# All of the second routed layer's shared expert beside the scatter, and the combination of routed results alone behind the expert loop

## The reference

```python
def _L1_ffn_ref(x, sg_w, su_w, sd_w, router_w, routing_bias, wg, wu, wd):
    xt = x.reshape(-1, H)
    shared = jax.nn.silu(xt @ sg_w.T) * (xt @ su_w.T) @ sd_w.T
    logits = xt @ router_w.T + routing_bias
    probs = jax.nn.sigmoid(logits)
    topk_p, topk_idx = jax.lax.top_k(probs, TOP_K)
    topk_p = topk_p / jnp.sum(topk_p, axis=-1, keepdims=True)
    ...
    h = jax.nn.silu(g) * u
    y = jnp.einsum('tei,ehi->teh', h, wd)
    routed = jnp.einsum('te,teh->th', w, y)
    return (shared + routed).reshape(orig_shape)
...
x = x + jnp.tanh(g_ffn[1]) * _L1_ffn_ref(_layernorm(x, axis=-1), ...)
```

## Time and profile before

| what | value |
|---|---|
| median of 3 runs | 1859.33 us (1855.94 to 1867.62) |
| the profiled execution | 1858.6 us |
| its span, first to last instruction | 1856.8 us |
| mean granted clock of TensorE | 0.878 of full speed |
| PE busy | 1455.4 us (78% of the span) |
| DVE, ACT, POOL busy | 1087.2, 894.4, 698.4 us |

### The profile page before, as it was taken

How to read it: one execution, slowest core, us unless ns; L and a number is a source line. 1 busy time by engine, 2 the same in 40 slices (tenths; PEclk the granted TensorE clock), 3 DMA queues, 4 the chain that set the end, 5 groups by cost and what they waited for, 6 DMA issues and landing times. The chain is left out here.

```text
span 1856.8 us, 31205 instructions
## 1 busy us (share of the span) xinstructions
PE 1455.4 (78%) x10050; PEld 1280.1 (69%) x10050; DVE 1087.2 (59%) x2502; ACT 894.4 (48%) x1907; POOL 698.4 (38%) x678
## 2 busy tenths in 40 slices
PE   1699982399999999758998369999855944463898
PEld 0457772399999999635787359999854842153687
DVE  6356643277777777455755426777553456777444
ACT  4244440377777777325552126777423515454242
POOL 2222103454444454542212423444541840045244
PEclk8899985699999999879997679999988977785799
DMA  8000004256465565220001305777420010001001
GB/s 290 1 1 1 1 10 172 84 199 236 183 238 213 203 238 193 73 71 1 1 1 35 128 33 178 236 228 231 125 66 26 1 50 1 0 29 53 1 13 35
DMA packets 75565, 179.95 MB, mean 97 GB/s; under 512 B 11776, under 2 KB 58112, under 8 KB 66256
## 3 DMA queue, kind: packets, MB, share of 16 engines
q1 hardware_dynamic: 56816, 149.91, 23.2%
q0 software_dynamic: 6144, 16.79, 2.8%
q10 hardware_dynamic: 12512, 12.06, 1.9%
HBM read 150.16 MB, written 28.57 MB: 96 GB/s over the span
## 5 line engine op out<-in xcount | busy, mean ns | idle before, releaser
L1386 POOL TENSOR_TENSOR l0m_e_DL<-l0m_e_DN,l0m_e_DH 128x256 fp32r<-128x256 f32 x184 | 200.0, 1088 | 218.1 <-ACT l0m_e_DH L1257 218.1
L1204 PE MATMUL PS<-l0m_e_CH,l0m_e_UH 128*128 128x256 f32 x736 | 210.8, 286 | 1.5 <-DVE l0m_e_CL L1345 1.5
L1204 PE MATMUL PS<-l0m_e_CH,l0m_e_UL 128*128 128x256 f32 x736 | 209.0, 284 | 0.0
L1204 PE MATMUL PS<-l0m_e_CL,l0m_e_UH 128*128 128x256 f32 x736 | 208.9, 284 | 0.0
L1317 DVE TENSOR_TENSOR l0m_e_UL<-l0m_e_U,l0m_e_UH 128x512 fp32r<-128x512 f32 x184 | 126.9, 690 | 45.8 <-ACT l0m_e_UH L1248 45.8
L1386 POOL TENSOR_TENSOR l1m_e_DL<-l1m_e_DN,l1m_e_DH 128x256 fp32r<-128x256 f32 x92 | 96.3, 1047 | 151.7 <-ACT l1m_e_DH L1257 151.7
L1329 DVE SCALAR_TENSOR_TENSOR l0m_e_HR<-PS,l0m_e_BU,l0m_e_SG 128x256 f32<-128x256 f32 x184 | 89.1, 484 | 104.8 <-ACT l0m_e_SG L1265 103.6
L1204 PEld LDWEIGHTS PS<-l0m_e_CH,l0m_e_UH 128*128 128x128 f32 x736 | 142.0, 193 | 1.9 <-ACT l0m_e_UH L1248 1.9
L1204 PEld LDWEIGHTS PS<-l0m_e_CL,l0m_e_UH 128*128 128x128 f32 x736 | 141.9, 193 | 0.0
L1204 PEld LDWEIGHTS PS<-l0m_e_CH,l0m_e_UL 128*128 128x128 f32 x736 | 141.8, 193 | 0.0
L1248 ACT CAST l0m_e_UH<-l0m_e_U 128x512 fp32r<-128x512 f32 x184 | 112.5, 612 | 57.3 <-PEq L1486 57.2
(11 more groups left out here) (468 smaller groups left out, 4526.9 us busy)
## 6 DMA issues: line engine op xcount, KB each, us to landing
l0m_e_U<-in_l_up SPq DMA_DIRECT2D x23, 2048.0 KB, 8.2
l0m_e_DN<-in_l_down SPq DMA_DIRECT2D x23, 1024.0 KB, 5.0
l1m_e_U<-in_l_up SPq DMA_DIRECT2D x23, 1024.0 KB, 7.1
l1m_e_DN<-in_l_down SPq DMA_DIRECT2D x23, 512.0 KB
rows_by_expert<-ZERO SPq DMA_DIRECT2D x1, 5888.0 KB, 27.4
l0m_e_ROW<-rows_by_expert SPq DMA_DIRECT2D x23, 256.0 KB, 5.0
results_by_expert<-l0m_e_Y ACTq DMA_DIRECT2D x23, 256.0 KB, 2.1
l1m_e_ROW<-rows_by_expert SPq DMA_DIRECT2D x23, 256.0 KB, 3.8
```

The costliest lines, as they stand in the source:

```text
L1204: ins = nc.tensor.matmul(hb(f)[:, a * SLOTS:(a + 1) * SLOTS], w[:, f % RING, k, a, :], x[:, j, k, :], start=(p == 0), stop=(p == len(passe ...
L1386: nc.gpsimd.tensor_tensor(DL[:, f % RING, :], DN[:, j, f, :], DH[:, f % RING, :].bitcast(F32), ALU.subtract).then_inc(s_dl, 1)
```

## The change

The first run takes all 16 rows (eight blocks of 256 tokens, 32 units), still beside the scatter. The third stage is a block of its own, in which POOL gathers as before and DVE has nothing but the combination's 16 rows in order. The arguments and counters that interleaved the combination with the shared run are gone. In the new file lines behind the edit have other numbers: 1605 becomes 1614, 1589 becomes 1598, 1635 becomes 1644, and so on.

```diff
                         s_sc = sem("l1m_scattered")
-                        shared.run("l1m_sh1", 0, B // 2, split=(SU, SD), on_sp=weights.first_tiles,
+                        shared.run("l1m_sh", 0, B, split=(SU, SD), on_sp=weights.first_tiles,
                                    on_pool=lambda pool: scatter(pool, Z, SLOT, s_sc))
                     expert_tiles("l1m_e", weights)
                 combine = Combine(c, "l1m_c", W12, SLOT)
-                shared.run("l1m_sh2", B // 2, B, on_pool=combine.gather, combine=combine)
+                with nc.Block() as block:
+                    @block.gpsimd
+                    def _(pool):
+                        combine.gather(pool)
+
+                    @block.vector
+                    def _(dve):
+                        for b in range(B):
+                            combine.sequence(dve, b)
+                        combine.end(dve)
...
-            def run(self, tag, lo, hi, split=None, on_sp=None, on_pool=None, combine=None):
+            def run(self, tag, lo, hi, split=None, on_sp=None, on_pool=None):
...
-                            done, combined = 0, 0
...
-                                    done = n * R
-                                if combine is not None and combined < lo + done:
-                                    if combined >= lo:
-                                        dve.wait_ge(s_out, combined - lo + 1)
-                                    combine.sequence(dve, combined)
-                                    combined += 1
...
-                            if combine is not None:
-                                dve.wait_ge(s_out, BLOCKS * R)
-                                for b in range(combined, B):
-                                    combine.sequence(dve, b)
-                                combine.end(dve)
```

## The result

| kernel | median | runs |
|---|---|---|
| before | 1862.94 us (1855.94 to 1867.62) | 20 |
| changed | 1871.26 us (1862.62 to 1874.86) | 20 |

The ratio is 1.0045, with a 95% interval of 1.0035 to 1.0055: the change costs some 8.4 us (6.5 to 10.2). The profiled execution of the changed kernel took 1874.4 us (span 1872.6).

A forecast was written before the change was run, and what follows sets the result against it. It took PE's chain, restarted at about 1083 after the scatter, to bound the first stage, and PE's chain again behind the loop. +34.8 - 26.1 = +8.7 us on 1858.6 gives 1867.3, for the median 1868 us; range 1857 to 1880.

The forecast's parts named there:

- the likely case: Whole kernel: a time within 1% (18.6 us) of before, given 0.82.
- sum of +8.7: Whole kernel: +34.8 us ahead of the expert loop and -26.1 behind it, +10.4 at the other end.
- Six units meet the scatter as before: First shared run: the first four blocks keep their order and stall as before, the sixth SG near 1083.
- The added blocks cost 4 x 8.69 = 34.8 us: Ahead of the expert loop: four more blocks after the scatter, 8.69 us each, all on the path.
- the closing: End of the shared run: a wait for the last HL, then 24 down matmuls, there once in either kernel.
- The loop unchanged: Expert loop: starts at 1147 instead of 1112, its 220 us unchanged.
- The last stage shrinks by 26.1 us: Behind the loop: without shared work the stage goes from 70.35 to 44.3 us.
- a pitch: Last stage: gathers follow one another without a pause, 1.256 us apart.
- POOL's closing: End of the last stage: POOL might leave later than DVE, 1.7 us extra not taken, making -24.4 the other end.
- The second rival: Last stage: DVE's adds slow POOL's gathers to 1.68 us each, 22.6 us longer, 1891 us; 8 in 100.
- The third: Added blocks ahead of the loop: PE at 1.2 GHz costs 30 us more, 1898 us; 3 in 100.
- The first: First stage: units keep their own pace through the scatter, sum -19.5, 1840 us; 4 in 100.

The follow-up runs named there:

- the second pair: Both kernels run again unchanged in a new series: before 1859.01 us, changed 1869.42 us, ratio 1.0049.
- without standing: Series where the shared expert keeps its pace while POOL makes indirect transfers; the kernel before took 1811.96, 1815.89 and 1815.76 us.
- x_two: Kernel before, scatter replaced by 32 direct SP transfers, second shared run in blocks of 512 tokens: 1830.08 us, one run.
- e_late: Kernel before with DVE's order alone changed, the combination's 16 rows behind the second run's last shared output: 1840.20 us, ratio 1.0121.
- x_both: Kernel before, scatter replaced by 32 direct SP transfers, all of the combination behind the last shared output: 1833.36 us.
- e_tok512b: Kernel before with the shared expert in blocks of 512 tokens in both runs: 1818.20 us, ratio 1.0021.

## Why the prediction was right, point by point

It gave 1868 us with a range of 1857 to 1880, and within 1% as the likely case; 1871.26 was measured, and the ratio of 1.0045 is inside that case. Its sum of +8.7 met +7.55 in the profiled pair, +8.15 by the two stages of the second pair, and 8.4 in the medians.

- *Six units meet the scatter as before, the sixth near 1083.* Right: 46.5 us behind the block's start, 44.9 before.
- *The added blocks cost 4 x 8.69 = 34.8 us.* The distance of a block was 8.70. The stage grew by 33.56, 1.2 less. The sixth SG came 1.6 us later after the stage's start than before, the five units behind it took 10.92 us instead of 12.26, and the closing was 1.5 shorter, which the prediction had counted as the same, "partly at the lower clock". From the run's last SG to the loop's first load, windows of before, and then of after:

```profile
1105.31:1112.55 7.24, 4.60 (x24) 4.42 (x24) 2.58 (x7) 1.08 (x3) 0.00 (x0) 0.76 0.00 0
```

```profile
1144.87:1150.59 5.72, 3.08 (x24) 2.91 (x24) 2.58 (x7) 1.08 (x3) 0.00 (x0) 1.00 0.00 0
```

  The same 24 matmuls took 4.60 us at a granted 0.76 and 3.08 at 1.00. In the changed kernel PE had been working without a pause for longer when it came to them.
- *The loop unchanged.* 220.81 against 220.52.
- *The last stage shrinks by 26.1 us.* It shrank by 26.30 (from 70.91 to 44.61 us; the prediction's 70.35 and 44.3 are cut at the block's start and end). Its terms: a pitch of 1.254 (1.256 predicted), and 2.83 us from the last issue to the last add (2.7). From the last add's start to DVE's end it was 0.94 us; the 1.13 of the prediction reach to the stage's end. The next transfer came at 1416.01, 4.48 of which came from the layers ahead; without them 1411.5, 1412.7 predicted. From DVE's end at 1414.07 to that transfer it was 1.94 us, 1.68 before: of the 1.7 us that POOL's closing might have added 0.3 is seen.
- *The second rival, DVE holding up the gather.* It didn't come: with 30 adds beside 32 gathers the longest took 0.99 us (one of before took 1.68). So here DVE's operations with two inputs in SBUF cost POOL nothing that shows.
- *The third, the lower clock.* It didn't come. The window of five added and old blocks in the changed kernel has PE busy all through at a granted 1.00:

```profile
1099.90:1143.43 43.53, 43.53 (x362) 43.27 (x361) 21.11 (x54) 15.66 (x44) 0.00 (x0) 1.00 0.01 1
```

- *The first, units that pass the scatter at their own pace.* In the series of the result it didn't come. In the three without standing it did, and then its price was wrong by its sign: it gave 1840, 19.5 us under before, and measured was +21 over. The step that failed is that it let the scatter swallow units in the changed kernel only, and set that against a kernel before whose PE stands. What lets PE pass the scatter lets it pass in both kernels, and the gather too.

That last point bears on the reason given, "because PE there is already late behind the scatter and nothing is left to hide it". For the series of the result it holds, and x_two shows it from the other side: take POOL's indirect transfers away and the first four blocks take 43.5 us. One thing in it is read too simply: "PE is late". PE's own rows of before show the matmuls of all six units over by 1052.24, and then a pause until the down products, which wait for DVE's HL of the fourth unit:

```profile
1052.24 0.28 PE L1605 MATMUL PS<-l1m_sh_CH,l1m_sh_UL 128*128 128x256 f32 x1
...
1062.64 0.42 DVE L1654 TENSOR_TENSOR l1m_sh_HL<-l1m_sh_HR,l1m_sh_HH 128x256 fp32r<-128x256 f32 x1
...
1063.15 0.55 PE L1589 MATMUL PS<-l1m_sh_DH,l1m_sh_HH 128*128 128x256 f32 x1 [10.64 <-issue]
```

ACT began the fifth and the sixth SG at 1061.88 and 1082.92, 11 and 31 us behind the last matmul of their units as PE's rows have it, where e_late has 0.3 us. Only from 1068.21 on does PE itself show single matmuls with pauses between them. So what comes late first is ACT's start, or the signal that it waits for; or the rows of PE are too early. The trace doesn't tell which, and the sum needs only that the sixth SG comes with the end of the scatter.

But the standing is no property of the kernel. Without it the four added blocks aren't hidden either but for 4.8 us, since the first four have used up 43.5 of the scatter's 48.3 (x_both, e_late), and there the second run was cheap: 54 - 44.6 = 9.4 us of the last stage for 34.8 us of PE's work. The sign is the same in both kinds of series, the size isn't: +8 and +21 us. The prediction read its rows in one series and didn't ask whether they would look the same in another. That the result came from a series of the same kind was luck on this point: in one without standing it would have been +1.1%, outside the likely case.

On the Trainium skill's sentence in "SBUF — State Buffer", section "Who interferes with whom", that a DMA never contends with a compute engine: x_two with its direct transfers and all series without standing agree with it. The waits of 21.33 and 19.85 us for the sixth SG beside POOL's indirect transfers speak against it, though no run shows what it is that they wait for. By that sentence alone the forecast would have been the first rival's.

## What to carry to other kernels

Where work of one engine is hidden beside transfers of another, compare what it costs on either side of the border: here half of the shared expert cost 26 us beside the gather (9 in another series) and 34 ahead of the loop, where the cover was used up already. When a rival takes a stall away, take it away in both kernels before pricing it. And before a stall is called a property of the program, see the same instructions in a second series of runs: two stages here were 26 and, as worked out, some 17 us shorter there.

## What the runs showed that was not expected

- The same program takes some 1860 us in one series and some 1814 in another, with all runs of a series within 1% of each other. The difference is where POOL issues indirect transfers while PE has work: 74.5 against 48.3 us in the first stage (26), 71 against some 54 in the last (17), and 8.2 against 2.7 at the end of layer 0's gather (5.5); that is 48.7 together, about the whole difference. POOL's own pace is nearly the same in both: the first and the last scatter start 41.0 us apart in the earlier trace rows and 42.8 in e_late.
- It isn't bound to a chip's number: x_two (with standing) and e_tok512b (without) ran some four minutes apart on a chip of the same number. What is set anew from one series to the next, and why it makes PE late beside indirect transfers only, stays open.
- The traces of the two kinds differ in one more thing. The landings of layer 0's gather are on record in every trace without standing, so that the view of the transfers gives their median time, and it gives none in any trace with standing. First the line of before, then of e_late:

```profile
l0m_c_GA<-results_by_expert,l0m_SLOT POOLq DMA_INDIRECT x32
```

```profile
l0m_c_GA<-results_by_expert,l0m_SLOT POOLq DMA_INDIRECT x32, 2.7
```

  So some of these records are missing where the engines stand. Whether the recording itself makes them stand is a rival that no run tests. It also means that rows beside the scatter are to be read with care, PE's above all.
- Late in the scatter PE gets through single matmuls, with pauses of 2.43 us before and up to 2.45 in the changed kernel. Some 5 us behind POOL's last issue (1079.0 and 1083.5) it is back at its pace.
- A gather of 128 rows of 1 KB takes POOL 0.95 us and a step of 1.254 us with DVE's adds beside it. The first gathers of e_late, which have none beside them, step by 1.253.
